# Rings and issue order of the query and table scatters in the typed attention's tables

## The reference, cut to what matters

```python
def _L1_gnn_ref(h, k_linears, q_linears, v_linears, a_linears, relation_att, relation_msg, ...):
    ...                                    # 4 node types, 8 relations, 4 heads of 64
    k = _typed_matmul(h, k_linears, node_type).reshape(n, N_HEADS, D_K)
    q = _typed_matmul(h, q_linears, node_type).reshape(n, N_HEADS, D_K)
    v = _typed_matmul(h, v_linears, node_type).reshape(n, N_HEADS, D_K)
    q_att = jnp.einsum('nhd,rhde->rnhe', q, relation_att)
    v_msg = jnp.einsum('nhd,rhde->rnhe', v, relation_msg)
    aw_q_edge = q_att[etype, col_idx]
    msg_edge = v_msg[etype, row_idx]
    attn_score = jnp.sum(aw_q_edge * k[row_idx], axis=-1)
    ...
```

## Time and profile before

| | |
|---|---|
| median of 3 runs | 7190.42 us (7181.17 to 7193.0) |
| the profiled execution: its own time | 7201.72 us |
| its span, first to last instruction | 7200.0 us |
| busy share PE / DVE / ACT / POOL | 74% / 48% / 24% / 33% |
| mean granted TensorE clock | 0.816 of full speed |
| `hgt_tables` | about 2600 to 3030 us of the span |

### The profile page before, as it was taken

One profiled execution on the slowest core, in us unless ns is written; L12 is line 12 of the kernel. 1 busy time (PEld: TensorE's weight loads), 2 busy tenths in 40 slices (PEclk: granted clock), 3 DMA queues, 4 the chain that ended last, 5 costly groups with the idle time before them and its releaser, 6 DMA issues. The chain is left out here.

```text
span 7200.0 us, 94015 instructions
## 1 busy us (share of the span) xinstructions
PE 5353.2 (74%) x23560; PEld 3476.5 (48%) x23617; DVE 3481.6 (48%) x7116; ACT 1749.0 (24%) x4175; POOL 2390.4 (33%) x2714
## 2 busy tenths in 40 slices
PE   5958889577639967578886887999999676344567
PEld 2224455333317643244444566777777543244445
DVE  8879925455552122267776774223011403644443
ACT  1936520122102222111111013334222211200022
POOL 1759877155206111155551000000111011366600
PEclk8989999655558987778886897999999788677678
DMA  0004489111200034488875641000333131122300
GB/s 26 2 16 174 158 337 330 42 26 27 61 0 19 6 113 158 178 266 256 259 252 157 206 142 12 13 9 35 123 102 102 64 114 60 57 90 90 88 14 18
DMA packets 392707, 756.55 MB, mean 105 GB/s; under 512 B 108493, under 2 KB 229595, under 8 KB 388275
## 3 DMA queue, kind: packets, MB, share of 16 engines
q1 hardware_dynamic: 295274, 500.54, 20.8%
q0 software_dynamic: 97056, 253.68, 11.9%
q10 hardware_dynamic: 192, 0.15, 0.0%
HBM read 502.20 MB, written 251.98 MB: 105 GB/s over the span
## 5 line engine op out<-in xcount | busy, mean ns | idle before, releaser
L1807 POOL DMA_INDIRECT big<-hgt_table,edge_key x448 | 424.2, 947 | 384.2 <-DVE hgt_s_tmp L1911 243.2
L936 PE MATMUL wsum_a_ps<-wsum_a_hot,wsum_a_rows 128*128 128x128 f32 x1664 | 300.6, 358 | 328.4 <-DVE big L963 280.0
L505 POOL DMA_INDIRECT back_sorted<-back_space x391 | 393.8, 1007 | 448.9 <-issue 447.4
L922 POOL DMA_INDIRECT wsum_a_rows<-table,edge_src x416 | 427.5, 1028 | 311.2 <-ACTq L914 126.3
L2859 POOL CAST sagel_piece<-x 128x1600 fp32r<-128x1600 f16 (+1 forms) x75 | 112.5, 1500 | 1016.9 <-DMA x<-counts 573.6
L936 PEld LDWEIGHTS wsum_a_ps<-wsum_a_hot,wsum_a_rows 128*128 128x128 f32 x1664 | 282.6, 266 | 346.4 <-DVE big L963 294.4
L2915 PE MATMUL sagel_ps<-sagel_piece,sagel_high 128*128 128x512 f32 (+1 forms) x1050 | 400.2, 389 | 0.8 <-issue 0.8
L1901 DVE TENSOR_REDUCE hgt_highest<-hgt_s_pm 128x512 f32 (+1 forms) x448 | 305.6, 685 | 170.3 <-PE hgt_s_pm L1856 95.1
L1807 POOL DMA_INDIRECT big<-gat_table,own_src x288 | 272.7, 947 | 335.5 <-issue 221.1
L505 POOL DMA_INDIRECT own_sorted<-big x256 | 284.3, 1110 | 293.0 <-issue 292.1
L2915 PE MATMUL sagel_ps<-sagel_piece,sagel_low 128*128 128x512 f32 (+1 forms) x1050 | 381.5, 377 | 0.0
(11 more groups left out here) (944 smaller groups left out, 11601.7 us busy)
## 6 DMA issues: line engine op xcount, KB each, us to landing
hgt_edge_values<-big SPq DMA_DIRECT2D x112, 512.0 KB
big<-hgt_edge_values SPq DMA_DIRECT2D x112, 512.0 KB, 3.9
x<-counts SPq DMA_DIRECT2D x75, 400.0 KB, 3.1
big<-counts SPq DMA_DIRECT2D x23, 1280.0 KB
x<-counts SPq DMA_DIRECT2D x75, 384.0 KB, 3.1
big<-hgt_e_ends SPq DMA_DIRECT2D x112, 256.0 KB
counts<-big SPq DMA_DIRECT2D x25, 832.0 KB
counts<-big SPq DMA_DIRECT2D x25, 768.0 KB
```

The costliest lines, as they stand in the source:

```text
L505: self.nc.gpsimd.indirect_dma_start(self.e.dram, bass.IndirectOffsetOnAxis(ap=self.adr[:, c:c + 1], axis=0), self.rec[:, c, :], None).then ...
L922: nc.gpsimd.indirect_dma_start(rows[n % DEEP][:, u, :], None, table, bass.IndirectOffsetOnAxis(ap=e.src[:, g:g + 1], axis=0)).then_inc(gat ...
L936: mm = nc.tensor.matmul(ps[r.slot % 2][u][:, k * P:(k + 1) * P], rows[r.slot][:, u, k * P:(k + 1) * P], hot[r.slot % 2][:, u, :], start=Tr ...
L1807: nc.gpsimd.indirect_dma_start(rows[n % DEEP][:, u, :], None, at.table, bass.IndirectOffsetOnAxis(ap=at.index[:, g:g + 1], axis=0)).then_i ...
```

## The change

The queries get five buffers and five semaphores, the table's output rows three (the third is newly allocated, the other two are the same spaces as before). GpSimd's order becomes: five gathers, the query scatters of tiles 0 and 1, and then for tile o the gather of tile o+5, the query scatter of tile o+2, and the table scatter of tile o. The copy of the queries of tile p waits for the scatter of tile p-5; the copies into `out` of tile o wait for the table scatter of tile o-3. At the end GpSimd waits for eight semaphores rather than four. What is computed, and what TensorE, ScalarE and VectorE issue, is otherwise unchanged.

```diff
--- before.py
+++ after.py
@@ -2561,12 +2561,13 @@
 
 
     TILES = order.tiles
-    AHEAD = 5
+    AHEAD, QUERIES, OUT = 5, 5, 3
     with ExitStack() as c:
         def many(count, name, shape):
             return [c.enter_context(nc.sbuf_tensor(f"hgtt_{name}{n}", shape, F32)) for n in range(count)]
         xs, xt = many(AHEAD, "xs", [P, D]), many(2, "xt", [P, 2, P])
-        kv, kvt, qs = many(2, "kv", [P, 2 * D]), many(2, "kvt", [P, 2 * HP, P]), many(2, "qs", [P, D])
+        kv, kvt, qs = many(2, "kv", [P, 2 * D]), many(2, "kvt", [P, 2 * HP, P]), many(QUERIES, "qs", [P, D])
+        space = [*space, *(a[:] for a in many(OUT - len(space), "out", [P, RELS * 2 * D]))]
         out = [a.rearrange("p (r d) -> p r d", r=RELS) for a in space]
         px, pq, pkv, pt = (c.enter_context(nc.psum_tensor(f"hgtt_p{n}", [P, 512], F32)) for n in ("x", "q", "kv", "t"))
         pr = [c.enter_context(nc.psum_tensor(f"hgtt_pr{n}", [P, 512], F32)) for n in range(4)]
@@ -2574,7 +2575,7 @@
             nc, c, "hgtt", "turned x_copied projected kv_copied q_copied kv_turned kvt_copied k_out v_out")
         related = sems(nc, c, "hgtt", "related_low related_high")
         gathered = gather_sems(nc, "hgtt", "gathered", AHEAD)
-        q_sent, out_sent = (gather_sems(nc, "hgtt", n, 2) for n in ("q_sent", "out_sent"))
+        q_sent, out_sent = gather_sems(nc, "hgtt", "q_sent", QUERIES), gather_sems(nc, "hgtt", "out_sent", OUT)
 
         parts = [(v, hp, h2) for hp in range(HP) for v, h2 in ((0, 0), (1, 1), (0, 1), (1, 0))]
 
@@ -2587,13 +2588,13 @@
 
         def copy_out(copy, eng, o, mine, done):
 
-            if o >= 2:
-                eng.wait_ge(out_sent[o % 2], 16 * (o // 2))
+            if o >= OUT:
+                eng.wait_ge(out_sent[o % OUT], 16 * (o // OUT))
             for n, (v, hp, h2) in enumerate(parts):
                 if v == mine:
                     eng.wait_ge(related[h2], o * each + nth[n])
                     at = v * D + hp * P + h2 * DK
-                    copy(out[o % 2][:, :, at:at + DK], pr[n % 4][:].rearrange("p (r n) -> p r n", r=RELS)).then_inc(done, 1)
+                    copy(out[o % OUT][:, :, at:at + DK], pr[n % 4][:].rearrange("p (r n) -> p r n", r=RELS)).then_inc(done, 1)
 
         with nc.Block() as block:
             @block.gpsimd
@@ -2606,18 +2607,27 @@
                         if o >= AHEAD:
                             pool.wait_ge(turned, o - AHEAD + 1)
                         nc.gpsimd.indirect_dma_start(xs[o % AHEAD][:], None, rows, where(order.source, o)).then_inc(gathered[o % AHEAD], 16)
+                def send_queries(o):
+                    if o < TILES:
+                        pool.wait_ge(q_copied, o + 1)
+                        nc.gpsimd.indirect_dma_start(q_rows, where(order.at, o), qs[o % QUERIES][:], None
+                                                     ).then_inc(q_sent[o % QUERIES], 16)
                 for o in range(AHEAD):
                     gather(o)
+                for o in range(2):
+                    send_queries(o)
+
                 for o in range(TILES):
                     gather(o + AHEAD)
-                    pool.wait_ge(q_copied, o + 1)
-                    nc.gpsimd.indirect_dma_start(q_rows, where(order.at, o), qs[o % 2][:], None).then_inc(q_sent[o % 2], 16)
+                    send_queries(o + 2)
                     pool.wait_ge(k_out, (o + 1) * each)
                     pool.wait_ge(v_out, (o + 1) * each)
-                    nc.gpsimd.indirect_dma_start(table, where(order.at, o), space[o % 2], None).then_inc(out_sent[o % 2], 16)
-                for n in range(2):
-                    pool.wait_ge(q_sent[n], 16 * ((TILES + 1 - n) // 2))
-                    pool.wait_ge(out_sent[n], 16 * ((TILES + 1 - n) // 2))
+                    nc.gpsimd.indirect_dma_start(table, where(order.at, o), space[o % OUT], None
+                                                 ).then_inc(out_sent[o % OUT], 16)
+                for n in range(QUERIES):
+                    pool.wait_ge(q_sent[n], 16 * ((TILES + QUERIES - 1 - n) // QUERIES))
+                for n in range(OUT):
+                    pool.wait_ge(out_sent[n], 16 * ((TILES + OUT - 1 - n) // OUT))
 
             @block.tensor
             def _(pe):
@@ -2691,9 +2701,9 @@
                 def step(x, p, k, r):
                     if p is not None:
                         dve.wait_ge(projected, p + 1)
-                        if p >= 2:
-                            dve.wait_ge(q_sent[p % 2], 16 * (p // 2))
-                        nc.vector.tensor_copy(qs[p % 2][:], pq[:, 0:D]).then_inc(q_copied, 1)
+                        if p >= QUERIES:
+                            dve.wait_ge(q_sent[p % QUERIES], 16 * (p // QUERIES))
+                        nc.vector.tensor_copy(qs[p % QUERIES][:], pq[:, 0:D]).then_inc(q_copied, 1)
                     if k is not None:
                         dve.wait_ge(kv_turned, k + 1)
                         if k >= 2:
```

## The result

The changed kernel takes 6984.1 us (median of 4 runs, 6980.52 to 6985.39) against 7185.8 us for the kernel before (median of 4, 7169.38 to 7193.0). The ratio is **0.972, with an interval of 0.970 to 0.974**: 202 us, or 2.8%, faster. The profiled execution took 6985.39 us.

What follows compares the result with a forecast made beforehand. One stage was held to be bound by a loop through the queries' landing behind the table scatter; 25 tiles x (15.21 - 7.26) us = 198.8 us off the 7190.4 us median gave 6992 us, range 6972 to 7042.

Steps and rivals of the forecast that it cites:

- The bound: Stage at 2600 to 3030 us: table issue to queries' landing 8.15 us, then 6.98 to next table; 15.21 a tile.
- The new pace: Tile step without landing waits: 3.39 us turnings and projections plus 3.87 us relation products, 7.26 us a tile.
- rival A: TensorE sets the stage's pace at full clock, 7.1 to 7.8 us a tile, 203 to 185 us gained; chance 0.77.
- B: Transfers set the pace if tables do not overlap: 9.1 us a tile, 153 us gained, 7038 us; chance 0.08.
- C: Short bank waits bring TensorE's clock back to 0.78: 9.3 us a tile, 148 us gained, 7043 us; chance 0.08.
- D: Another wait replaces this one or clock stays at 1.2 GHz: gain 0 to 18 us; chance 0.03.
- E: GpSimd's indirect DMA issues take up to 5.51 us each: 16.5 us a tile, 33 us slower, 7223 us; chance 0.04.
- The transfers' floor: The stage's 2.36 MB a tile at 393 GB/s take 6.0 us, below the 7.26 us step.
- The output row: Copies into the table's output rows: two buffers would just do; the third is credited with nothing by itself.
- The ends: Stage's start and end: four more waits, at most 1.2 us, against 0.7 us; taken as zero, 1.5 us either side.
- Outside the stage: All other stages unmoved; the prediction is wrong if they move by more than 10 us.

Runs made afterwards that it cites:

- table_scattered_twice: The changed kernel with every table output row also scattered into a second HBM table that nobody reads: ratio 0.986, 7079.7 us.
- projections_between: The changed kernel with TensorE's step reordered, the eight relation products split into two groups of four with other work between: ratio 0.972, 6979.8 us.
- third_row_alone: The kernel before with only a third output row added, query ring of two and old order kept: ratio 1.001.

## Why the prediction was right

The forecast was 6992 us, 198.8 us below the median; measured were 6984 us, 202 us below. By its own steps:

- *The bound.* The loop from the table's issue over the queries' landing and VectorE back to the next table's issue was the cause: with either the ring or the order changed it is gone, and with neither, it stays at 15.2 us a tile.
- *The new pace.* 7.26 us were taken from the one step without a wait; measured are 7.34. Single tiles take 7.25, 7.32 and 7.44 us. Over 25 tiles this is 2 us less gain than reckoned: 196.9 us.
- *Who sets it.* TensorE, at the full clock (1.00, 170.00 of 170 us busy), as rival A had it. B fell with tables that overlap at 416 GB/s, C with a clock that stays at 1.00, D and E with GpSimd's issues at 0.97 us and no new wait.
- *The transfers' floor.* Reckoned 6.0 us at 393 GB/s, measured 5.7 at 416. DMA share and rate came as foretold, 0.82 and 321 GB/s for "near 0.8" and "near 320".
- *The output row.* "Two would just do" holds in the tiles (7.33 us with two rows). At the end it does not: there the third row gives some 2.3 us.
- *The ends.* Taken as zero with 1.5 us to either side; from tile 25's issue to the next stage it was 3031.34 - 3005.09 = 26.3 us and is 25.2 us: 1.1 us gained. With 0.1 us at the start, 196.9 + 1.1 + 0.1 = 198.1 us. The table scatters there are now 4.51 and 4.18 us apart, so the 5.92 and 5.70 us which the prediction gave as a sign of the transfers' pace say little of it: the first ended with VectorE's copies, and the second held a wait of 2 us for an output row, which the third row takes away. The transfers' floor itself is borne out by `table_scattered_twice`.
- *Outside the stage.* "Unmoved" holds by the medians as far as they can tell (3.6 us, with 13 us to either side), but in a single pair of profiles the rest differed by 18 us, more than the 10 us that I had set as the mark of being wrong. The mark was too tight: for such a pair the spread of the kernel before, 7169 to 7193 us, is 24 us.

The 3.87 us of the relation products were taken "with all waits for banks in it", and so they stayed: the change does not touch these waits, and the step took them over whole. That is why a pace counted from one step held for 25, and it did not need the inside of that step to be understood. `projections_between` shows what lies in there: about 0.3 us are waits for banks, and taking them away by another order costs as much as it gives.

## What to carry to other kernels

When an engine waits for a DMA to land before it may reuse a small buffer, look at what stands ahead of that DMA in its queue: 128 KB of queries waited behind 2 MB of table, and a longer ring of buffers (five instead of two; three or four were not tried) or an earlier place in the queue removes the wait, either alone. Count a tile's time from one unstalled tile in the profile of before, if there is one; here it gave the new pace to 1%. And a wait on TensorE costs more than its length where the clock falls in it: here a fifth to a quarter of the gain, 1.65 to 1.8 of 7.9 us a tile, was work that ran at 1.2 GHz after the wait.

## What was not expected of the hardware

- More work made the kernel faster: five useless products a tile in an idle stretch of TensorE gave 0.9945 of the time.
- Chips differ by more than this change is worth, though not in the stage that it touches. In the group with `third_row_alone` the kernel before took 6803 us, against 7186 us in the group of the result; the stage took 429.3 us in `third_row_alone` itself, against 429.2 in the kernel before. Times of different groups must not be compared; the changed kernel's ratio was 0.972 in both groups that had it.
- Changing between kinds of work costs TensorE time at the full clock: a second group of relation products in a tile cost about 0.2 us at its ends and 0.2 us in the projections beside it, more than the 0.3 us that the emptied banks gave.
- The table's rows, 16 KB each to scattered places in HBM, were written at 416 GB/s together with the small scatters and gathers, and for 250 us on end.
